# Attention B's maxima: placements a set at a time and two of them on ACT's queue; in FFN1 the factors of B's weights behind the second gate choice

## The reference

```
x = x + attn_a(layernorm(x))     # 32 heads of 128, 8 KV heads, int4-like weights
x = x + ffn(layernorm(x))        # "FFN1"
x = x + attn_b(layernorm(x))     # 32 heads of 16, 8 KV heads: "attention B"
x = x + ffn(layernorm(x))

def ffn(x):                      # 8 experts of rank 64, the best 2 of each token
    gate_probs = softmax(x @ gate_w.T)
    weights, sel = top_k(gate_probs, 2); weights = weights / sum(weights)
    return sum over e of w_full[:, e] * (x @ lora_A[e].T @ lora_B[e].T)

def attn_b(x):
    q, k, v = x @ Wq, x @ Wk, x @ Wv            # then rotary factors on q and k
    att = where(causal, q @ k.T / sqrt(16), -inf)
    return (softmax(att) @ v) @ Wo
```

## Time and profile before

| what | value |
|---|---|
| median of 3 runs | 951.85 us (951.2 to 951.88) |
| the profiled execution | 950.79 us |
| its span, first to last instruction | 949.1 us |
| mean granted share of TensorE's clock | 0.995 |
| busy share of the span | PE 96%, DVE 81%, POOL 65%, ACT 63% |

### The profile page before, as it was taken

How to read it: one execution, slowest core, us unless ns; L and a number is a source line. 1 busy time by engine, 2 the same in 40 slices (tenths; PEclk the granted TensorE clock), 3 DMA queues, 4 the chain that set the end, 5 groups by cost and what they waited for, 6 DMA issues and landing times.

```text
span 949.1 us, 19791 instructions
## 1 busy us (share of the span) xinstructions
PE 912.1 (96%) x6698; PEld 487.6 (51%) x6698; DVE 771.8 (81%) x1812; ACT 598.8 (63%) x1323; POOL 618.9 (65%) x668
## 2 busy tenths in 40 slices
PE   5889999999999999999999999999999989999998
PEld 3445555555555555545555555554445534444543
DVE  6888887887887788788788878898878879996764
ACT  4677666676667567666576756646463469997331
POOL 4788876968777687687777777822368744553211
PEclk9999999999999999999999999999999999999999
DMA  9177376484665556647557465464332943121145
GB/s 339 51 182 173 87 185 145 63 211 107 122 186 88 144 116 157 144 86 199 117 101 190 83 144 144 87 175 84 76 82 55 163 80 64 42 43 24 23 86 159
DMA packets 256005, 114.10 MB, mean 120 GB/s; under 512 B 244144, under 2 KB 244784, under 8 KB 251312
## 3 DMA queue, kind: packets, MB, share of 16 engines
q1 hardware_dynamic: 246416, 70.42, 39.1%
q10 hardware_dynamic: 9504, 42.49, 12.9%
HBM read 49.84 MB, written 2.10 MB: 55 GB/s over the span
## 4 chain that ended last, share of the span: by engine, by line
PE 76%; DVE 10%; ACT 6%; issue 3%; DMA 3%; POOL 1%; SPq 1%; ACTq 0%; DVEq 0%; POOLq 0%
PE bank L1253 16%; PE bank L1255 16%; PE bank L1254 16%; PE bank L1734 4%; PE bank L1352 3%; PE bank L1354 3%; PE bank L1353 3%; PE bank L1372 3%; PE bank L1374 3%; PE bank L1373 3%; ACT bank L989 2%; PE bank L1666 2%; DVE bw_hi L1981 2%; DVE bank L1964 2%; PE bank L1640 2%
## 5 line engine op out<-in xcount | busy, mean ns | idle before, releaser
L622 POOL TENSOR_TENSOR rt<-rt 128x512 f32<-128x512 f32 x80 | 101.6, 1273 | 131.8 <-DVE rt L1949 131.8
L1981 DVE SCALAR_TENSOR_TENSOR bw_hi<-bank,rden,bw_hi 128x128 f16<-128x128 f32 (+3 forms) x256 | 123.3, 544 | 60.9 <-ACT bw_hi L1025 60.9
L989 ACT ACTIVATE bank<-bank,shift,c_score 128x128 f32<-128x128 f32 (+3 forms) x256 | 147.3, 605 | 2.1
L1964 DVE CUSTOM_DVE_ANT_0 bank<-bank,mask_w 128x512 f32<-128x512 f32 (+3 forms) x256 | 117.9, 520 | 21.5 <-PE bank L1354 21.5
L1025 ACT ACTIVATE bw_hi<-bank,rden 128x128 f16<-128x128 f32 (+3 forms) x256 | 114.5, 535 | 22.4 <-DVE rden L1974 22.2
L984 ACT ACTIVATE shift<-smax,c_score 128x4 f32<-128x4 f32 x64 | 19.0, 297 | 155.4 <-DVE smax L1964 155.4
L629 POOL TENSOR_TENSOR arena<-rt,arena 128x512 f16<-128x512 f32 x80 | 92.4, 1158 | 8.6 <-ACT arena L973 7.8
L1253 PE MATMUL bank<-xt,wq_hi 128*128 128x512 f16 x256 | 97.0, 379 | 0.0
L1254 PE MATMUL bank<-xt,wq_hi 128*128 128x512 f16 x256 | 97.0, 379 | 0.0
L1255 PE MATMUL bank<-xt,wq_lo 128*128 128x512 f16 x256 | 97.0, 379 | 0.0
L1253 PE MATMUL bank<-wo_hi,arena 128*128 128x512 f16 x256 | 97.0, 379 | 0.0
(11 more groups left out here) (241 smaller groups left out, 2453.6 us busy)
## 6 DMA issues: line engine op xcount, KB each, us to landing
qcode<-in_q_codes ACTq DMA_DIRECT2D x7, 1024.0 KB, 5.0
qscale<-in_q_scales ACTq DMA_DIRECT2D x7, 1024.0 KB, 7.2
ocode<-in_o_codes ACTq DMA_DIRECT2D x7, 1024.0 KB, 4.9
oscale<-in_o_scales ACTq DMA_DIRECT2D x7, 1024.0 KB, 7.9
kvcode<-in_k_codes ACTq DMA_DIRECT2D x8, 256.0 KB, 7.5
kvcode<-in_v_codes ACTq DMA_DIRECT2D x8, 256.0 KB, 7.9
kvscale<-in_k_scales ACTq DMA_DIRECT2D x8, 256.0 KB, 8.1
kvscale<-in_v_scales ACTq DMA_DIRECT2D x8, 256.0 KB, 8.9
```

The costliest lines, as they stand in the source:

```text
L989: act.activation(a_rows(i, s), a_rows(i, s), ACT.Exp, bias=shift[:, s % 2, c:c + 1], scale=c_score[:, 0:1], accum_out=bank[3][:, SUMS_AT + ...
L1964: dve.tensor_tensor_reduce(bank[bk][:, o:o + (i + 1) * P], bank[bk][:, o:o + (i + 1) * P], mask_w[:, S - (i + 1) * P:S], 1.0, LOWEST, ALU. ...
L1981: dve.scalar_tensor_tensor(out=p_row[:, s % 2, LO_AT[i]:LO_AT[i] + P_STEP * i + 1:P_STEP], in0=turned_back(i, s), scalar=rden[:, s % 2, c: ...
```

## The change

It has two parts that don't touch each other.

In attention B, from set 2 on, SP places both pairs of a set together: two DMAs of 2 x 2 x 512 elements instead of four of 2 x 512, behind the landing of both pairs' transposes (`place_set`). PE's keys of such a set wait once, at step 0, for both DMAs. In sets 0 and 1 pairs are still placed apart; pair 0 by SP, pair 1 by ACT on its own queue: set 0's behind its second exponential, set 1's behind all exponentials of set 0. With that, SP's big transposes of queries 6 and 7 move ahead: tile 6 stands now before `turn_max(1, 0)`, tile 7 after `turn_max(1, 1)` with no placement behind it. Semaphores are named apart for the first two sets (`d_mfirst`), so that the counts of the others start at set 2.

In FFN1, DVE's `w_factors(1)` stands behind `gate_choice(ph, 1)` instead of ahead of `rows_low(ph, 0)`.

```
+        def max_turned(q, c):
+            return (d_mfirst[c][q], 16) if q < 2 else (d_mturn[c], 16 * (q - 1))
+
+        def place_max(eng, q, c):
+            j, b = set_place(q)
+            eng.wait_ge(*max_turned(q, c))
+            for f in range(2):
+                two = slice(f * P // 2 + MAX_AT, f * P // 2 + MAX_AT + 2)
+                eng.dma_start(qt_b[two, 2 * j + c, b * S:(b + 1) * S], m_turned[two, q % 2, c]
+                              ).then_inc(d_mrows[c][q], 16)
...
             def turn_max(q, c):
                 sp.wait_ge(bsplit_done, 2 * q + c + 1)
-                if q >= 2:
-                    sp.wait_ge(d_mrows[c][q % 2], 32 * (q // 2))
+                if q >= 4:
+                    sp.wait_ge(d_mset[q % 2], 32 * (q // 2 - 1))
+                elif q >= 2:
+                    sp.wait_ge(d_mrows[c][q % 2], 32)
...
+            def place_set(q):
                 j, b = set_place(q)
-                sp.wait_ge(d_mturn[c], 16 * (q + 1))
+                for c in range(2):
+                    sp.wait_ge(*max_turned(q, c))
                 for f in range(2):
                     two = slice(f * P // 2 + MAX_AT, f * P // 2 + MAX_AT + 2)
-                    sp.dma_start(qt_b[two, 2 * j + c, b * S:(b + 1) * S], m_turned[two, q % 2, c]
-                                 ).then_inc(d_mrows[c][q % 2], 16)
+                    sp.dma_start(qt_b[two, 2 * j:2 * j + 2, b * S:(b + 1) * S], m_turned[two, q % 2]
+                                 ).then_inc(d_mset[q % 2], 16)
...
             for q in range(SETS + 2):
-                if q < SETS:
+                if q == 0:
+                    b_exps(q, range(2))
+                    place_max(act, q, 1)
+                    b_exps(q, range(2, LOADS - 2))
+                elif q < SETS:
                     b_exps(q, range(LOADS - 2))
                 if 1 <= q <= SETS:
                     b_ctx_out(q - 1)
                 if q < SETS:
                     b_exps(q, range(LOADS - 2, LOADS))
+                if q == 0:
+                    place_max(act, 1, 1)
...
-                if step in (0, 2):
-                    pe.wait_ge(d_mrows[step // 2][q % 2], 32 * (q // 2 + 1))
+                if q < 2 and step in (0, 2):
+                    pe.wait_ge(d_mrows[step // 2][q], 32)
+                elif step == 0:
+                    pe.wait_ge(d_mset[q % 2], 32 * (q // 2))
...
                 gate_weights(ph, 0)
-                if ph == 0:
-                    w_factors(1)
                 rows_low(ph, 0)
                 rows_low(ph, 1)
                 gate_choice(ph, 1)
+                if ph == 0:
+                    w_factors(1)
                 gate_weights(ph, 1)
```

More of the change, by code:

```diff
@@ L430, in build @@
         d_mrows = [[sem(f"d_mrows{c}{i}") for i in range(2)] for c in range(2)]
+        d_mset = [sem(f"d_mset{i}") for i in range(2)]
+        d_mfirst = [[sem(f"d_mfirst{c}{i}") for i in range(2)] for c in range(2)]
         d_q, d_k = ([sem(f"{n}{i}") for i in range(2)] for n in ("d_q", "d_k"))
@@ L526, in turn_max @@
                 sp.wait_ge(bsplit_done, 2 * q + c + 1)
-                if q >= 2:
-                    sp.wait_ge(d_mrows[c][q % 2], 32 * (q // 2))
+                if q >= 4:
+                    sp.wait_ge(d_mset[q % 2], 32 * (q // 2 - 1))
+                elif q >= 2:
+                    sp.wait_ge(d_mrows[c][q % 2], 32)
                 sp.dma_start_transpose(m_turned[:, q % 2, c].rearrange("p (i n) -> p i n", n=P),
-                                       m_stack[:, q % 2, c].rearrange("p i n -> p (i n)")).then_inc(d_mturn[c], 16)
-            def place_max(q, c):
+                                       m_stack[:, q % 2, c].rearrange("p i n -> p (i n)")).then_inc(max_turned(q, c)[0], 16)
+            def place_set(q):
                 j, b = set_place(q)
-                sp.wait_ge(d_mturn[c], 16 * (q + 1))
+                for c in range(2):
+                    sp.wait_ge(*max_turned(q, c))
                 for f in range(2):
                     two = slice(f * P // 2 + MAX_AT, f * P // 2 + MAX_AT + 2)
-                    sp.dma_start(qt_b[two, 2 * j + c, b * S:(b + 1) * S], m_turned[two, q % 2, c]
-                                 ).then_inc(d_mrows[c][q % 2], 16)
+                    sp.dma_start(qt_b[two, 2 * j:2 * j + 2, b * S:(b + 1) * S], m_turned[two, q % 2]
+                                 ).then_inc(d_mset[q % 2], 16)
             sp.wait_ge(stacks_set, 2)
@@ L545, in _ @@
             turn_max(0, 0)
-            place_max(0, 0)
+            place_max(sp, 0, 0)
             turn_max(0, 1)
-            place_max(0, 1)
+            turn_queries(NT - 2)
             turn_max(1, 0)
-            turn_queries(NT - 2)
-            place_max(1, 0)
+            place_max(sp, 1, 0)
             turn_max(1, 1)
             turn_queries(NT - 1)
[L554 to L559, removed]
+            for q in range(2, SETS):
                 turn_max(q, 0)
                 turn_max(q, 1)
-                place_max(q, 0)
-                place_max(q, 1)
-                if q < 5:
+                place_set(q)
+                if 3 <= q < 5:
                     turn_keys(NT - 5 + q)
@@ L840, in b_split @@
                 if q >= 2:
-                    pool.wait_ge(d_mturn[c], 16 * (q - 1))
+                    pool.wait_ge(*max_turned(q - 2, c))
                 pool.tensor_tensor(low, m, max_dn[:].unsqueeze(1).broadcast_to([P, ST, 2]), ALU.mult).then_inc(bsplit, 1)
```

## The result

| | before | after |
|---|---|---|
| median | 951.2 us (950.11 to 955.25, 11 runs) | 954.67 us (952.35 to 957.19, 11 runs) |
| ratio | | 1.0033, 95% interval 1.0019 to 1.0047 |
| profiled execution, its span | 950.79, 949.1 us | 957.19, 955.5 us |

I had said 948.4 and 0.71 for faster. The kernel is about 3.1 us slower (951.2 x 0.0033), and a ratio of 1 lies outside the interval.

A forecast was written before the change was run, and what follows sets the result against it. In steady sets PE, DVE and ACT run in step, so only idle stretches could give time. FFN1 -1.2, ramp -2.4, set 5 -0.9, steady sets +1.0 made -3.5: 951.85 to 948.4 us, eight-in-ten range 945.8 to 951.3.

The forecast's parts named there:

- The steady sets: Attention B: pair 0 waits for pair 1's transpose; 0.7 late events at 1.4 us each, +1.0 us, bounds 0 and +3.
- FFN1: Moving the factors lets tile 0 land earlier and removes PE's 2.0 us wait: -1.2 us, bounds 0 and -2.2.
- The ramp: Attention B's start: set 1 begins as now, set 2 at 778.0 instead of 780.42: -2.4 us, bounds 0 and -2.6.
- Set 5: Attention B: fewer SP issues for sets 3 and 4 cut the wait to 0 to 0.6: -0.9 us, bounds 0 and -1.2.
- The slower one: Attention B: joint placement takes e more, each set from 5 on costs (e - 0.3)/2; 958.4 us at e 2.3; chance 0.09.
- Rival 3: FFN1 gives nothing because the half clock or DVE takes it back: -2.3, 949.5 us; chance 0.13.
- the steady sets over 6.8 apart: Attention B: sign that the prediction is wrong; it expected ACT's steady sets 6.75 us apart.

The follow-up runs named there:

- experiment 4: Also `e_set`: kernel before, with only sets 2 to 15 placed by two wide DMAs for both pairs; 955.2 us, ratio 1.0049.
- experiment 5: Kernel before, sets 2 to 15 placed by four narrow DMAs, none issued before both pairs' transposes landed; 967.52 us, ratio 1.0172.
- experiment 7: Kernel before with wide placements for sets 2 to 15, plus 64 more small matmuls at program start to shift instruction fetches; 958.6 us, ratio 1.0064.
- experiment 1: Kernel before with only the move of `w_factors(1)` in FFN1; 951.58 us, ratio 1.001.
- e_act: Kernel before with the new ramp's ACT placements but SP's old order of transposes; 951.15 us, ratio 1.0007.
- e_best2: Second run of the changed kernel with sets 2 to 15 placed pair by pair as before (new ramp, factors moved); 949.83 us, ratio 0.9995.
- e_ramp: Kernel before with the new ramp alone, FFN1 as before and pair by pair placement from set 2 on; 948.56 us, ratio 0.998.

## Why the prediction was wrong

**The steady sets: this step failed.** I wrote: "this one event costs 4.0 - 2.3 - 0.3 = 1.4. I take 0.7 such events: +1.0 us, bounds 0 and +3 (two events)". It measured +4.7 in time (experiment 4), and 3.6 of it between sets 3 and 14 of the trace. The mechanism was the one I named, a late transpose that pair 0 now waits for; experiment 5 shows that the wait costs without the width, and experiment 7 that the waits move with the late transposes. What failed is the count. I took it from the extremes of one view, "2.3/2.3/4.0", and one long placement. The landings one by one, which the trace had, show eight of the 24 transposes of sets 4 to 15 over 2.5 us already before the change. Three of them were pair 1's, in sets 4, 5 and 10, and those are what pair 0 now waits for. Before, only set 5 waited; the 1.4 us to spare, and the later need of pair 1, hid the others. The change used up 1.1 of the 1.4, and the width some 0.2 more. Five sets had a late pair 1 in the trace after it. Four of them waited that hadn't, for 0.7 to 1.0 us each: four events and not 0.7, though each was cheaper than my 1.4. And 13.2 of 13.5 us leave no room to win back any of it.

**The fall of the clock at set 14** was in no term. I had listed falls behind the two large old waits, and not asked what a new 1.6 us wait brings. In this trace it brought 1.5 us more. By "TensorE: Matmul & The Clock Gate" of the Trainium skill (Part 1) idleness brings the fall. The traces agree only in part, for the same 2.0 us wait in FFN1 had a fall behind it in five of nine executions.

**FFN1: mis-sized, and with the wrong sign on average.** I gave -1.2 with bounds 0 and -2.2. It measured +0.9 (-0.2 to +2.0). PE's side went as I wrote, step by step: 0.2 in place of the 2.0 at the first tile, 1.6 at the third, full clock. DVE's side did not. `gate_choice(1)` and the factors took what I said, but the remainders of tiles 0 and 1 took 0.85 and 1.00 where they had 0.68, and `rows_low(2)` began 0.76 later than before (I had 0.2 to 0.6). Then tile 3's remainder took 1.45 (702.24), where a trace with the old place and no fall (`e_set`) has 0.69. POOL's multiplication for the next tile was running when it began:

```profile
702.09 1.04 POOL L783 TENSOR_TENSOR hs<-hidden,wfull 128x512 f32<-128x512 f32 x1 [4.30 <-DVE m_stack L2233]
```

It ended at 703.13, and the remainder 0.55 behind it. That is no accident of one row. In the 14 traces 69 of these remainders are longer than 0.72 us. Each began while an instruction of POOL ran, and each ended 0.55 behind that instruction's end. Those that began with POOL idle took 0.68 to 0.69. So the price of a remainder hangs on where it falls against POOL, and I had taken 0.68 for all. The 1.3 us against `e_set` are then: tile 4's remainder starts 0.4 later behind the anchor and takes 1.38 instead of 1.15, and the last one takes 1.49 instead of 0.85. And I compared with a trace in which the clock had fallen, and took it for the normal case.

**The ramp: the right mechanism, and a size that luck helped.** Set 1 came at the same distance, set 2 nearer by 2.7, of which 0.3 is FFN1's: -2.4, as in the sum. But the trace before has one of its falls of the clock inside set 1. The trace of experiment 1 has the same ramp and a clock of 1.00 from 770 to 785:

```profile
773.60 2.53 ACT L1006 ACTIVATE pt<-bank,c_score_b 128x512 f32<-128x512 f32 x4 [2.31 <-PE bank L1666]
...
781.92 5.14 ACT L1006 ACTIVATE pt<-bank,c_score_b 128x512 f32<-128x512 f32 x8
```

There sets 1 and 2 are 8.32 apart and not 9.38. Behind the anchor set 2 begins at 87.51 there, at 89.04 in the trace before, and at 86.33 after the change. So the ramp itself gave 1.2 at set 2 (87.51 - 86.33), and the rest of the 2.4 was the fall, which doesn't come in every execution. It is the same mistake as in FFN1. In time the ramp alone gave -1.9 and -1.6, each within some 1.3, which tells neither size from the other. Nor did ACT's placement of set 1 land as early as I had it: it was issued from 772.28 on and landed at 775.9, 3.6 later, where I had taken 2.4 (769.8 to 772.2). PE waited 0.21 for it. "Trainium Kernel Development and Optimization" of the Trainium skill (Key Constraints) says that a second queue saves only issue time. The traces agree in part: this landing came late, and alone, in `e_act`, the second queue gave no time that can be told from none, but with the new order of SP it did.

**Set 5: the wait did not shrink** (1.29 against 1.22), where I had -0.9. In the kernels with the new ramp and pair by pair placement it was anything from 0.39 (`e_best2`) to 1.21 (`e_ramp`).

**The rivals.** The slower one had the right place but the wrong price: it took the width e for the cost, which is about 0.2 by issue and landing, below the 0.3 to spare, and at that e it gives no cost at all. Rival 3's ground came true, that DVE takes back what FFN1 has to give; its time of 949.5 didn't. Of what was to show me wrong, the steady sets over 6.8 apart came (7.5 to 7.9 at four of them). In sum, by the traces: -0.3 - 2.4 + 5.4 + 0.7 behind set 15 = +3.4. The last 0.7 I have not traced further.

## What to carry to other kernels

Where two transfers are joined so that both wait for the later one, price it by the whole distribution of the landing times, each with the spare time of the buffer it fills, and not by the median and one extreme. In a pipeline whose engines run in step with 0.3 us to spare, each late event is lost for good, while the same event behind 1.4 us of slack costs nothing. A short idle stretch of PE in the trace of before may have a fall of the clock behind it that comes only in every second execution: look at more than one trace before booking its removal as a gain. And a DVE instruction that is moved may land beside one of POOL and take twice its time.

## What was not expected of the hardware

- A DMA transpose of 128 x 512 elements lands after 2.3 us, and after up to 4.5 us when an instruction packet of 16 KB (or at times 8 KB) falls into its flight. In sets 4 to 15, in all 14 traces, each one over 2.5 us whose landing is recorded had such a packet in its flight. A packet of 16 KB comes every 6 to 12 us there. Moving the packets moved the late landings (experiment 7). By what path a packet on one DMA engine delays the transpose no run here shows.
- After the same wait of 2.0 us PE's clock fell to 1.2 GHz for 3.4 us in five of nine traces. Falls come in untouched stretches too, and the anchor ahead of the change moved between 691.4 and 694.4 from trace to trace. What decides whether one comes is open.
- DVE's remainders of 128 x 512 (two operands from SBUF) took 0.68 to 1.50 us. A long one always ended 0.55 us behind the end of the POOL instruction that ran when it began, be it the multiplication of the hidden rows or one on B's weights (69 of 69). One that began before POOL's wasn't stretched.
